# Reordering the opening and the first block of a fused attention and mixture-of-experts kernel

## What is computed

```python
pooled = pool(x, prompt_type)                    # masked softmax over the sequence, per token
x = x + attention(pooled)                        # 16 heads of 8, a shared rotary part of 32, causal
c = x @ W[cat_ids] + b[cat_ids]                  # a 128x128 weight per sequence, chosen from 64
w = route(c)                                     # sigmoid gate; best 4 of 8 groups, best 8 of 64 experts
y = sum over e of w[e] * ((silu(c @ Wg[e]) * (c @ Wu[e])) @ Wd[e])
out = x + y + (silu(c @ Wsg) * (c @ Wsu)) @ Wsd  # one shared expert on top
```

## Time and profile before

| | |
|---|---|
| median of 3 runs | 723.68 us (723.67 to 724.1) |
| the profiled execution, its own time | 725.9 us |
| its span, first to last instruction | 724.0 us |
| busy share of the span: PE, DVE, ACT, POOL | 96%, 75%, 61%, 59% |
| mean granted clock of PE | 0.992 |
| first gate product of block 0 / block 1 | 45.1 us / 145.2 us |
| first gate product of blocks 2 to 7 | 229.3, 313.9, 398.8, 483.6, 568.3, 649.5 us |

### The profile page before, as it was taken

The page is one execution under the profiler, slowest core; times in us unless marked ns, Lnnn a source line. Parts: engine busy times, 40 slices in busy tenths (PEclk is TensorE's granted clock), DMA queues, the critical chain, the costliest instruction groups (busy, mean ns, idle before and its releaser), DMA issues.

```text
span 724.0 us, 15734 instructions
## 1 busy us (share of the span) xinstructions
PE 697.4 (96%) x5606; PEld 544.1 (75%) x5606; DVE 544.5 (75%) x1146; ACT 442.7 (61%) x857; POOL 425.6 (59%) x351
## 2 busy tenths in 40 slices
PE   7878899899999999999999999999999999999997
PEld 5656677677887778777787778877787777887885
DVE  5777669686697787887688865976878876886664
ACT  3865865477555865478455675558654685565554
POOL 3626696865555655566455654566455664666665
PEclk9989999999999999999999999999999999999999
DMA  8272554345344445435544464444465344355441
GB/s 269 75 285 81 154 131 117 89 123 154 104 130 111 139 106 130 138 101 155 116 110 131 117 149 109 127 114 143 107 126 144 92 146 123 108 127 146 129 131 45
DMA packets 65117, 92.93 MB, mean 128 GB/s; under 512 B 7696, under 2 KB 26576, under 8 KB 65040
## 3 DMA queue, kind: packets, MB, share of 16 engines
q1 hardware_dynamic: 61008, 87.06, 44.5%
q10 hardware_dynamic: 4032, 4.87, 1.9%
HBM read 88.37 MB, written 3.15 MB: 126 GB/s over the span
## 4 chain that ended last, share of the span: by engine, by line
PE 70%; ACT 8%; DVE 8%; SPq 6%; issue 4%; DMA 2%; POOL 1%; POOLq 0%; DVEq 0%
PE banks L1026 68%; DVE hid L984 2%; SPq L316 2%; SPq L310 2%; ACT banks L543 2%; ACT s_t L424 2%; DVE hid L1002 2%; PE banks L1108 1%; ACT L543 1%; DVE k_blk L710 1%; ACT hid_hi L555 1%; ACT L424 1%; DMA gbias<-in_gate_bias 1%; DVE pt_sb L685 1%; POOL hid_lo L657 1%
## 5 line engine op out<-in xcount | busy, mean ns | idle before, releaser
L657 POOL TENSOR_TENSOR hid_lo<-hid,hid_hi 128x512 fp32r<-128x512 f32 (+1 forms) x264 | 343.3, 1300 | 255.8 <-ACT hid_hi L555 253.9
L984 DVE TENSOR_TENSOR hid<-banks,cwb 128x512 f32<-128x512 f32 x252 | 173.2, 687 | 117.1 <-ACT banks L543 114.4
L543 ACT ACTIVATE banks<-banks 128x512 f32<-128x512 f32 x252 | 146.1, 582 | 129.6 <-PE banks L1026 127.9
L555 ACT CAST hid_hi<-hid 128x512 fp32r<-128x512 f32 (+1 forms) x264 | 162.6, 616 | 79.3 <-DVE hid L1002 78.6
L1002 DVE TENSOR_TENSOR hid<-hid,banks 128x512 f32<-128x512 f32 (+1 forms) x262 | 180.0, 687 | 27.9 <-PE banks L1026 5.8
L1026 PE MATMUL banks<-c_hi,wg_hi 128*128 128x512 f32 x264 | 119.0, 451 | 5.6 <-POOL wu_lo L622 2.3
L1026 PE MATMUL banks<-hid_hi,wd_hi 128*128 128x512 f32 (+1 forms) x264 | 104.6, 396 | 0.8 <-POOL hid_lo L657 0.8
L1026 PE MATMUL banks<-c_hi,wu_hi 128*128 128x512 f32 x256 | 102.0, 398 | 2.3 <-DVE hid L1002 2.3
L1026 PE MATMUL banks<-c_hi,wg_lo 128*128 128x512 f32 x264 | 103.5, 392 | 0.0
L1026 PE MATMUL banks<-c_lo,wg_hi 128*128 128x512 f32 x264 | 103.5, 392 | 0.0
L1026 PE MATMUL banks<-hid_lo,wd_hi 128*128 128x512 f32 (+1 forms) x264 | 103.4, 392 | 0.0
(11 more groups left out here) (160 smaller groups left out, 799.6 us busy)
## 6 DMA issues: line engine op xcount, KB each, us to landing
cwb<-cw_scratch SPq DMA_DIRECT2D x254, 256.0 KB, 3.8
k_blk<-in_cond_w SPq DMA_DIRECT2D x112, 64.0 KB
xf<-in_x_feat SPq DMA_DIRECT2D x8, 256.0 KB, 4.0
out_feat<-y ACTq DMA_DIRECT2D x8, 256.0 KB, 3.6
wg_raw<-in_we_gate SPq DMA_DIRECT2D x3, 512.0 KB, 7.5
wu_raw<-in_we_up SPq DMA_DIRECT2D x3, 512.0 KB, 8.0
wd_raw<-in_we_down SPq DMA_DIRECT2D x3, 512.0 KB, 9.4
xf<-in_x_tok SPq DMA_DIRECT2D x6, 256.0 KB, 2.8
```

Source lines behind the costliest of these rows:

```text
L543: nc.scalar.activation(dst, gate_bank(p)[:, :], ACT.Silu).then_inc(S["silu_done"], 1)
L555: nc.scalar.copy(hid_hi[0:n, slot(b, p), :], hid[0:n, slot(b, p), :]).then_inc(S["hi_ready"], 1)
L657: nc.gpsimd.tensor_sub(hid_lo[0:n, slot(b, p), :], hid[0:n, slot(b, p), :], hid_hi[0:n, slot(b, p), :].bitcast(F32)).then_inc(S["lo_ready" ...
L984: nc.vector.tensor_mul(hid[:, slot(b, p), :], gate_bank(p)[:, :], cwb[:, p % NCW, :])\
```

## The change

It has these parts.

1. SP loads `cat_row` earlier, ahead of the tokens of blocks 1 to 3, with a semaphore of its own (`row_in`), and SP and DVE wait for that instead of `cats_in`. PE waits for the rest of `cats_in` at the product with `cat_table`.
2. Block 0's residual is loaded from ACT's queue, after `pooled_out(0)`, and no longer by SP behind the category weights.
3. ACT: splits 0 and 1 move from step 4 to step 10, `pooled_out(1)` from step 18 to 19, `pool_exp(2)` from step 19 to 21. DVE: `pool_weights(1)` moves from step 9 to 16, `spread(1)` from 16 to 18 (behind the residual addition). PE: `pool_out(1)` moves from step 18 to 19, the rotary product of block 1 from 19 to 20.
4. PE in front of the first routing weights: 1 `warm` product call instead of 7, and block 1's scores (step 6) are made there instead of behind unit 1. DVE and POOL do step 6 ahead of their first unit too. The second of the first banks is G1 instead of A1, which brings a wait for `silu_done` 4 on PE, and at the gate of unit 5 a wait for `hid_ready` 2.
5. `SPLITS`: 17 places, three of every four units from 6 to 24, then 26 and 27; before 6 to 17 and 24 to 28.
6. The shared expert's down product is stacked: its low part goes to rows 64 to 127 of `hid_hi`, its weights are loaded twice, and two products of PE do for three. POOL waits for its own previous subtraction there.
7. At the end, DVE makes the low parts of units 31 and 32 of the last block, POOL none of them. The last addition is made in two halves, stored by ACT and by SP.

The diff, cut to its core (the new semaphore's name and ACT's copy of the doubled shared weights are left out):

```diff
@@ -173,12 +173,12 @@
         first_scores = [A2, A1, G0, G1]
-        first_bank = [Y, A1]
+        first_bank = [Y, G1]
@@ -211,8 +211,8 @@
-        TWO_TILES = {0: [], 1: [6, 7], 2: [], 3: [8, 9], 4: []}
-        SECOND_ROUND = {3: [], 4: [8]}
+        TWO_TILES = {0: [], 1: [7], 2: [], 3: [8, 9], 4: []}
+        SECOND_ROUND = {1: [], 3: [], 4: [8]}
@@ -242,7 +242,7 @@
         BEFORE_UNITS = 8
-        SPLITS = {**{p: p + 2 for p in range(6, 18)}, 24: 20, 25: 21, 26: 22, 27: 23, 28: 24}
+        SPLITS = {p: i for i, p in enumerate((6, 7, 8, 10, 11, 12, 14, 15, 16, 18, 19, 20, 22, 23, 24, 26, 27), BEFORE_UNITS)}
         CHAIN = 21
@@ -275,9 +275,9 @@
             sp.dma_start(xt_in[0].rearrange("p (t d) -> p t d", d=D), x_tok[:, 0:TILES, :]).then_inc(S["xt_in0"], 16)
+            sp.dma_start(cat_row[:, :], cats.to_broadcast([CATS, NSEQ])).then_inc(S["row_in"], 16)
             for i in range(1, 4):
                 sp.dma_start(xf_in[i], x_feat[:, bass.ts(i, TOK)]).then_inc(S["x_in1"], 16)
-            sp.dma_start(cat_row[:, :], cats.to_broadcast([CATS, NSEQ])).then_inc(S["cats_in"], 16)
             sp.dma_start(cat_table, cond_b).then_inc(S["cats_in"], 16)
@@ -323,17 +323,17 @@
             token_load(1, "xt_in1")
-            sp.wait_ge(S["cats_in"], 48)
+            sp.wait_ge(S["row_in"], 16)
             for p in range(9, 17):
                 attention_loads(p, 0)
-            attention_loads(0, 0)
             for m in range(3):
...
             sp.dma_start(wg_raw[:, NPAIR, :], ws_gu).then_inc(S["ws_in"], 16)
-            sp.dma_start(wd_raw[0:F, NPAIR, :], ws_down).then_inc(S["ws_in"], 16)
+            for i in range(2):
+                sp.dma_start(wd_raw[F * i:F * i + F, NPAIR, :], ws_down).then_inc(S["ws_in"], 16)
             sp.wait_ge(S["c2tok_ps"], 1)
@@ -359,7 +359,9 @@
             pipeline(unit_loads)
-            sp.wait_ge(S["y_free"], 16 * NBLK + 16)
+            sp.wait_ge(S["y_ready"], NBLK + 2)
+            sp.dma_start(out[:, bass.ts(2 * NBLK - 1, TOK // 2)], y[:, TOK // 2:TOK]).then_inc(S["y_free"], 16)
+            sp.wait_ge(S["y_free"], 16 * NBLK + 32)
@@ -507,15 +509,15 @@
             pooled_out(0)
+            act.dma_start(xf[:, :], x_feat[:, 0:TOK]).then_inc(S["res_in"], 16)
             for p in range(CWT):
                 attention_step(p, 0)
-                if p == 4:
-                    split(0)
-                    split(1)
-                elif p == 8:
+                if p == 8:
                     pool_exp(1)
...
                     pool_hidden(2)
+                    split(0)
+                    split(1)
                     split(2)
@@ -523,14 +525,13 @@
                     split(5)
-                elif p == 18:
+                elif p == 19:
                     pooled_out(1)
-                elif p == 19:
                     split(6)
-                    pool_exp(2)
                 elif p == 20:
...
                 elif p == 21:
+                    pool_exp(2)
                     split(7)
@@ -592,7 +593,7 @@
             act.wait_ge(S["y_ready"], NBLK + 1)
-            act.dma_start(out[:, bass.ts(NBLK - 1, TOK)], y[:, :]).then_inc(S["y_free"], 16)
+            act.dma_start(out[:, bass.ts(2 * NBLK - 2, TOK // 2)], y[:, 0:TOK // 2]).then_inc(S["y_free"], 16)
@@ -643,18 +644,24 @@
                 if p == 20:
-                    pool.wait_ge(S["cats_in"], 48)
+                    pool.wait_ge(S["cats_in"], 32)
                 attention_step(p, 0)
...
                 split(i)
+            attention_step(6, 1)
             def unit(b, p, par, following, last, prev):
+                if b == NBLK - 1 and p >= NPAIR - 1:
+                    return
                 pool.wait_ge(S["hi_ready"], b * UNITS + p + 1)
                 n = P if p < NPAIR else F
-                nc.gpsimd.tensor_sub(hid_lo[0:n, slot(b, p), :], hid[0:n, slot(b, p), :],
+                if p == NPAIR or (p == 0 and b):
+                    pool.wait_ge(S["lo_ready"], b * UNITS + p)
+                rest = hid_lo[:, slot(b, p), :] if p < NPAIR else hid_hi[F:2 * F, slot(b, p), :]
+                nc.gpsimd.tensor_sub(rest, hid[0:n, slot(b, p), :],
                                      hid_hi[0:n, slot(b, p), :].bitcast(F32)).then_inc(S["lo_ready"], 1)
@@ -926,7 +933,7 @@
             spread(0)
-            dve.wait_ge(S["cats_in"], 48)
+            dve.wait_ge(S["row_in"], 16)
             setup(nc.vector.tensor_copy(onehot, cat_row[:, :]))
@@ -942,11 +949,10 @@
                     pool_scores(1)
-                elif p == 9:
+                elif p == 16:
                     pool_weights(1)
-                elif p == 16:
+                elif p == 18:
                     spread(1)
-                elif p == 18:
                     pool_scores(2)
@@ -1012,10 +1018,27 @@
+            def last_rests():
+
+                dve.wait_ge(S["hid_ready"], NBLK * UNITS)
+                for p in range(NPAIR - 1, UNITS):
+                    n = P if p < NPAIR else F
+                    at = slot(NBLK - 1, p)
+                    rest = hid_lo[:, at, :] if p < NPAIR else hid_hi[F:2 * F, at, :]
+                    dve.wait_ge(S["hi_ready"], (NBLK - 1) * UNITS + p + 1)
+                    dve.wait_ge(S["lo_ready"], (NBLK - 1) * UNITS + p)
+                    nc.vector.tensor_sub(rest, hid[0:n, at, :], hid_hi[0:n, at, :].bitcast(F32)).then_inc(S["lo_ready"], 1)
+
             gate_up(0)
             gate_up(1)
+            attention_step(6, 1)
             pipeline(unit)
-            total(NBLK - 1)
+            last_rests()
+            dve.wait_ge(S["down_done"], NBLK * UNITS)
+            dve.wait_ge(S["x2_moved"], NBLK)
+            for i in range(2):
+                part = bass.ts(i, TOK // 2)
+                nc.vector.tensor_add(y[:, part], Y[:, part], y[:, part]).then_inc(S["y_ready"], 1)
@@ -1080,8 +1103,6 @@
                         pe.wait_ge(S["k_ready"], blk * HG + HG)
-                        if blk == 1:
-                            pe.wait_ge(S["hid_ready"], 2)
                     else:
@@ -1235,10 +1256,11 @@
                     pe.wait_ge(S["onehot_ready"], 1)
+                    pe.wait_ge(S["cats_in"], 32)
                     mm(Y[:, P:2 * P], cat_table, onehot).then_inc(S["cat_ps"], 1)
-                elif p == 18:
+                elif p == 19:
                     pool_out(1)
-                elif p == 19:
+                elif p == 20:
                     pe.wait_ge(S["pooled_ready"], 2)
@@ -1251,12 +1273,15 @@
                 pe.wait_ge(S["cat_read"], 1)
-                warm(7, Y)
+                warm(1, Y)
                 attention_step(CWT, 0)
+                attention_step(6, 1)
                 pe.wait_ge(S["cwT_ready"], 1)
...
                 for u in range(2):
+                    if u == 1:
+                        pe.wait_ge(S["silu_done"], 4)
                     dst = first_bank[u].rearrange("p (u two n) -> p two u n", two=2, n=P)
@@ -1269,7 +1294,6 @@
             def down(b, p):
-                n = P if p < NPAIR else F
                 pe.wait_ge(S["lo_ready"], b * UNITS + p + 1)
@@ -1277,8 +1301,13 @@
                     pe.wait_ge(S["y_ready"], b + 1)
-                three(Y[:, :], wd_hi[0:n, p, :], wd_lo[0:n, p, :], hid_hi[0:n, slot(b, p), :], hid_lo[0:n, slot(b, p), :],
-                      p == 0, p == UNITS - 1).then_inc(S["down_done"], 1)
+                if p == NPAIR:
+                    mm(Y[:, :], wd_hi[:, p, :], hid_hi[:, slot(b, p), :], start=False, stop=False)
+                    last = mm(Y[:, :], wd_lo[0:F, p, :], hid_hi[0:F, slot(b, p), :], start=False, stop=True)
+                else:
+                    last = three(Y[:, :], wd_hi[:, p, :], wd_lo[:, p, :], hid_hi[:, slot(b, p), :], hid_lo[:, slot(b, p), :],
+                                 p == 0, False)
+                last.then_inc(S["down_done"], 1)
@@ -1288,8 +1317,10 @@
                     pe.wait_ge(S["hid_ready"], b * UNITS + (p - 1))
-                elif b == 0 and p in (2, 3, 4, 5):
+                elif b == 0 and p in (2, 3, 4):
                     pe.wait_ge(S["silu_done"], p - 1)
+                elif b == 0 and p == 5:
+                    pe.wait_ge(S["hid_ready"], 2)
                 else:
```

6 lines of the change are left out of this document (3 added, 3 removed).

## The result

The changed kernel took 720.25 us in the median of 5 runs (716.79 to 720.86), the kernel before 723.68 (5 runs, 723.0 to 724.79): a ratio of 0.9942 with a 95% interval of 0.992 to 0.9964. That is 3.4 us faster where 11.4 were forecast, and outside the range given. The profiled execution took 720.5 us by its own time, with a span of 718.7 against 724.0. Block 1 starts at 142.16 us, and the forecast had called itself failed behind 139.

The account below looks back on a forecast made before the run. PE, busy 697.4 of 724.0 us, was taken to bound the kernel. Gains of 2.8 + 2.1 + 3.6 + 1.6 + 1.3 = 11.4 us from 723.7 gave 712.3 us; range from near 708.5 to 717.5.

Parts of the forecast that it names:

- term 2: Block 0's first routing weights: one warm call for seven stores them 2.1 us sooner, and so units 4 to 13.
- term 3: Block 0, units 18 to 30: new split places leave 2.0 of 5.64 us lost, gain 3.6; bounds 0 and 5.6.
- Term 1: Opening: residual load on ACT's queue lets the addition wait for the projection instead; gain 2.8 us, bounds 1.0 and 3.9.
- near 55: Block 0: sign of being right, the first load of routing weights issued near 55 us, 59.84 before.
- Rival A: Splits beside routing make DVE the bound of units 18 to 26; the 5.64 us stay lost, 715.9 us; chance 0.20.
- three such hits: Units 17 to 19: DVE routing operations lengthened beside splits, costing units 20 and 21 0.7 us each.
- forecast's 29.7: Block 0: sign of being right, about 29.7 us from unit 18 to 30, 33.29 before.
- Term 4: Shared expert's down product: one matmul fewer on PE in seven blocks, gain 1.6 us, bounds 1.4 and 1.8.
- Term 5: Tail: last products end 1.1 us sooner, halved addition and smaller store 0.2; gain 1.3 us, bounds 0.8 and 1.6.
- B: Opening: DVE held up ahead of c2, clock falls onto products with `pick`; 1.0 + 1.0 for 4.9, 715.2 us; chance 0.16.
- C: Units 4 to 12: with six warm calls gone the clock stays at 1.2 GHz; 13.5 us more, 725.8; chance 0.04.
- D: Opening: residual load waits behind 1.5 MB of weights, costing at most 2.8 us; chance 0.02, shared with several passed lower bounds.

Follow-up runs that it names:

- first trace: The changed kernel with no further edit, profiled at the first measurement against the kernel before: 720.25 us, ratio 0.9942, span 718.7.
- second: The changed kernel run again with no edit, in the first set of experiments: 718.8 us, ratio 0.9922, span 716.7.
- third: The changed kernel run a third time with no edit, in the third set of experiments: 720.1 us, ratio 0.9949, span 717.2.
- scores back, splits sooner: The changed kernel with block 1's scores back behind unit 1 and splits at units 6 to 17 and 23 to 27: 716.37 us, ratio 0.9917.

## Why the prediction was right and wrong

Three things failed: the way from the copy of the first routing weights to their store (term 2), the loss that the new places of the splits leave (term 3), and the trace that the sum was taken from, whose low stretches it counted as gain. The table shows how much sooner than in the trace of before each point is reached, in us (before: 45.10, 59.84, 106.46, 139.75, 715.20, 724.0):

| point | forecast | first trace | second | third | scores back, splits sooner |
|---|---|---|---|---|---|
| first gate product | 2.8 | 0.1 | 2.8 | 2.9 | 2.7 |
| first load of weights | 4.9 | 0.6 | 3.3 | 3.6 | 5.1 |
| gate of unit 18 | 4.9 | 1.1 | 3.0 | 3.9 | 5.7 |
| gate of unit 30 | 8.5 | 3.0 | 4.9 | 4.3 | 8.9 |
| last gate product | 10.1 | 4.4 | 6.3 | 5.8 | 10.3 |
| end of the span | 11.4 | 5.3 | 7.3 | 6.8 | 11.2 |

The last column reaches the forecast, but only against the trace that the forecast was worked out from. That execution took 725.9 us and had three low stretches; seven runs of the kernel before with a mean clock of 1.00 took 721.2 to 722.35. The mended kernel's trace has no low stretch at all. By this estimate about 4 us of the 11.2 are the clock of the two executions and not the change, and the sum took them for a gain: it used durations and waits of one execution at 725.9 and subtracted the result from a median of 723.7.

**Term 1, the opening: right in mechanism and size (2.8), wrong about how often.** Addition 34.34, c2 39.28, first gate 42.33, all as worked out (the projection's two products take 1.13 us in the earlier trace rows, not 0.9; no term hangs on it). What the step left out is that its base, the trace of before, had clock 1.00 in front of the scores. In the first trace of the changed kernel the low level fell there and took 2.7. I had treated the low stretches as part of the program's order ("PE's idle stretch of 36 to 38 us is gone"); three executions of one program show the first of them at 12, 50 and 68 us. Also, the part of the term that came from reordering the pooling is nothing in the trace with the load alone, which has its first gate product at 42.14.

**Term 2, the first routing weights: the step that failed.** "One warm call for seven: ... 2.1 us for the store, and so for units 4 to 13." The copy did come as forecast (54.37 for 54.45); two other things were wrong. First, the copy is not the store, and this is what was lost in the measured kernel: I priced block 1's scores on PE ("I count nothing more") and not in the DMA engines, where one code packet of PE beside the two stores makes copy to load 4.83 to 4.95 us for 3.28 in five of ten traces, and 3.76 to 3.97 in the others. Second, the 2.1 hold only at the low clock: the warm matmuls took 3.19 us in the earlier trace rows at 0.50. At 1.00 it is 1.71 us from cw to the copy with seven calls (the kernels with only the load moved and with seven kept) and 0.95 with one (scores back): the step is worth 0.8 there, and by the medians seven calls lose nothing that can be told (717.9 and 718.8; 716.78 and 716.37). From the first gate product to the first load the second trace gains 0.5 and not 2.1. The kernel with only the scores put back has the copy at 51.53 and the load at 54.81, and that is the "near 55" of the forecast. That the packet is there only with the moved scores, and the delay only with the packet, is shown in sixteen traces; that it holds the store by standing before it on the same DMA engine is my reading of the 9 late packets, which start as the code packet ends. That block 0 moves with the first load holds to a us or so: from it to the gate of unit 18 it takes 45.6 to 47.6 us in fifteen of the sixteen traces, and 49.1 in one.

The Trainium skill ("Runtime: NRT & Kernel Launch", section "Instruction fetch mechanics") says that each sequencer fetches its code by a DMA queue of its own in pieces of 16 KiB, and that crossing such a boundary is mostly hidden. The trace agrees with the size (44 packets, 0.72 MB) and with the engine being undisturbed (in the second trace PE is busy for the whole of 52 to 56 us); what is not hidden here is the other transfer that the piece meets.

**Term 3, the splits: half (1.95, or 0.4, for 3.6).** The wait at the gate of unit 28 is gone, as said. I took 2.0 us of loss left out of 5.64; 3.7 are left in six traces with the change's places and 5.2 in two. Rival A's mechanism is in the rows: in the second trace nine routing operations of units 18 to 26 take 0.69 to 1.39 us each beside POOL's subtractions, five of them (L807, L815, L830, L839, L846) beside a split and four (L788, L812, L827, L849) beside an ordinary `hid_lo`; and the gate of unit 24 waits 0.70 for the split of unit 20, whose end I had put level with it. The mechanism of A was right, its price between my two cases, and it swings by 1.6 us with a single hit of `hid_lo` (L790). That hit I had read wrongly: of the "three such hits" of the trace of before, which I took for splits, the third (1.28 us) stands beside `hid_lo`. The hit alone does not cost the 1.6 us: the four traces with units 18 to 22 free of splits all have it, and take 30.04 to 30.07.

The rule of the Trainium skill that the prediction quotes ("SBUF — State Buffer", section "Who interferes with whom") says that one of the two engines is blocked in full. The rows with two inputs in SBUF that were held agree (L807 1.39 for 0.28, L830 0.96 for 0.42); L790 does in ten traces, but in the other six it is not held, and POOL's subtraction takes 1.47 to 1.48 us where one with nothing beside it takes 1.30, so neither is blocked in full. L827 and L846, with one tensor input, were held too (0.78 and 0.97). The mended places, with units 18 to 22 free of splits and the last five one unit forward, come near the forecast's 29.7.

**Term 4, the shared product: right.** 1.3 us against the trace of before and 1.9 against the one with only the load moved, for 1.6; over all fourteen traces that have it, 1.0 to 1.6 and 1.5 to 2.1.

**Term 5, the tail: the mechanism right, the size 0.95 for 1.3.** DVE's second subtraction ends 713.99 + 0.68 = 714.67, 3.83 after the last gate product (710.84), as worked out (3.78). But the products behind it take until 715.66, 1.0 us and not 0.7, so the addition starts 4.86 after that gate product where it was 5.63: 0.8 for 1.1. The addition in halves and the smaller store give the other 0.2, as said.

**The other rivals.** B's mechanism (the low clock onto the products with `pick`) is in the first two traces: in the first they take 3.62 us at 0.50, and 1.99 in the kernel with the scores back at 1.00. Its other half, DVE held up ahead of c2, is not there (c2 4.8 and 4.9 us behind the addition, for 4.65 before). But with the clock up and the scores still moved (the warm calls in front of units 2 and 3) no clear gain came, so it is not what term 2 lost. C, the slower case, is not there: no trace has a low stretch longer than 7 us. D did not occur: the residual landed by 21.3 us in every trace that has its load on ACT's queue. The range was too narrow above for plain reasons: terms 2 and 3 could both lose most of their gain at once, which I had priced only one at a time (0.16 and 0.20), the clock's place was in no bound, and the sum was taken from an execution with three low stretches.

## What to carry to other kernels

Look at where the granted clock is low in the trace that a sum starts from, take what these stretches cost off the gain (here about 4 us of 11.4), and add as a bound that the low stretch falls onto a busy place in the next execution: here 2.7 us of a gain of 2.8. A step moved in front of a short, latency-bound transfer has to be looked at in the DMA view too, PE's own code among the packets. And where two engines hold each other up, as DVE and POOL do here, put the long operations where the other engine has few small ones, rather than evenly: leaving the routing alone and moving five splits by one unit took 1.3 us less in the traces than spreading them.

## What was not expected of the hardware

- One packet of PE's code amid two stores of 64 KB made the first load behind them 1.6 us later (4.83 to 4.95 us from the copy, for 3.28), though for 0.9 us of that nothing but the code packet was moving.
- The same program gets its low stretch of the clock in different places from one execution to the next: 11.7 to 18.5 and 52.6 to 59.5 us, 50.0 to 56.8, 68.1 to 75.0 in the three traces of the changed kernel.
- A VectorE operation of 128x32 elements that starts 0.13 us behind a GpSimd subtraction took 0.18 us in six traces and 1.28 to 1.29 in ten, with the same start. With the change's places of the splits that makes 1.6 us in twelve units (31.3 for 32.9).
